# Summing two node tables on TensorE instead of VectorE in one stage of a graph network kernel

## What is computed

```
h = jnp.maximum(_layernorm(x, axis=-1), 0.0)
x = x + _L2_gnn_ref(h, edge_attr_32, edge_index, ...)

# in _L2_gnn_ref
proj_edge = (node_attr @ W_node)[edge_neigh]
m_node = segment_sum(proj_edge * (edge_attr @ W_edge), edge_center, num_segments=num_nodes)
cat = concatenate([node_attr @ W_center_node, m_node], axis=-1)
h_node = _layernorm(cat @ W_concat_node, ln_weight, ln_bias)
```

## Time and profile before

| what | value |
|---|---|
| median of three runs | 5954.6 us |
| the profiled execution | 5969.23 us, its span 5967.4 us |
| the stage's first and last sum on DVE | 4326.0 and 4697.8 us into the span |
| PE, DVE, ACT, POOL busy, of the whole span | 3748.6, 3959.9, 2012.0, 3039.3 us |

### The profile page before, as it was taken

One profiled execution on the slowest core, in us unless ns is written; L12 is line 12 of the kernel. 1 busy time (PEld: TensorE's weight loads), 2 busy tenths in 40 slices (PEclk: granted clock), 3 DMA queues, 4 the chain that ended last, 5 costly groups with the idle time before them and its releaser, 6 DMA issues. The chain is left out here.

```text
span 5967.4 us, 85405 instructions
## 1 busy us (share of the span) xinstructions
PE 3748.6 (63%) x16668; PEld 2531.9 (42%) x16668; DVE 3959.9 (66%) x12622; ACT 2012.0 (34%) x4449; POOL 3039.3 (51%) x2764
## 2 busy tenths in 40 slices
PE   0788883333599985579965566666400199889830
PEld 0566662332367764544455545555300044334310
DVE  8555556887388863654455555656488788888856
ACT  0555542333122221235565632222144333333310
POOL 0655534777676600000077767777700367777730
PEclk9888885555799998999967778888855599999975
DMA  6677766776455545877677767777588511111149
GB/s 228 151 174 173 172 159 192 219 217 176 125 132 144 142 161 170 276 246 229 219 243 231 227 170 130 131 130 128 88 280 271 156 31 39 43 46 47 49 162 375
DMA packets 986574, 996.40 MB, mean 167 GB/s; under 512 B 210641, under 2 KB 648417, under 8 KB 986163
## 3 DMA queue, kind: packets, MB, share of 16 engines
q1 hardware_dynamic: 676899, 628.12, 37.1%
q0 software_dynamic: 131904, 146.31, 12.6%
q10 hardware_dynamic: 177488, 218.95, 10.3%
HBM read 560.95 MB, written 466.16 MB: 172 GB/s over the span
## 5 line engine op out<-in xcount | busy, mean ns | idle before, releaser
L709 POOL DMA_INDIRECT at_first_table<-n_h,n_first_edge x784 | 811.5, 1035 | 1247.3 <-ACT n_h L277 901.1
L2495 PE MATMUL e_m<-e_by_rel,rel_w 128*128 128x512 f32 x1568 | 718.3, 613 | 0.0
L701 POOL DMA_INDIRECT e_xs<-x_table,e_idx x392 | 377.6, 963 | 516.0 <-POOLq L2385 396.8
L701 POOL DMA_INDIRECT e_x<-x,e_idx x392 | 408.2, 1041 | 371.8 <-DMA e_idx<-idx_table 261.3
L701 POOL DMA_INDIRECT e_hs<-h_table,e_idx x392 | 423.3, 1080 | 170.3 <-issue 110.9
L2409 DVE SCALAR_TENSOR_TENSOR e_by_rel<-e_y,e_part_t 128x512 f32<-128x512 f32 x784 | 476.0, 678 | 31.4 <-PE e_y L2510 24.0
L709 POOL DMA_INDIRECT rel_sum_table<-e_res,e_again x392 | 392.6, 1001 | 148.6 <-issue 125.2
L2495 PEld LDWEIGHTS e_m<-e_by_rel,rel_w 128*128 128x128 f32 x1568 | 302.6, 198 | 346.6 <-issue 346.6
L277 ACT ACTIVATE n_h<-n_x,n_norm_shift,n_norm_rstd 128x128 f32<-128x128 f32 x784 | 321.8, 482 | 327.1 <-issue 266.2
L1014 PE MATMUL n_m<-n_mean,n_pick 128*128 128x129 f32 x784 | 204.7, 442 | 356.2 <-DVE n_pick L1079 352.7
L2487 PE MATMUL e_t<-ident,e_part 128*128 128x128 f32 x392 | 70.1, 307 | 561.0 <-ACT e_part L277 442.6
(11 more groups left out here) (373 smaller groups left out, 10428.9 us busy)
## 6 DMA issues: line engine op xcount, KB each, us to landing
x_table<-n_x ACTq DMA_DIRECT2D x294, 256.0 KB
n_x<-x_table SPq DMA_DIRECT2D x294, 256.0 KB
e_hd<-at_first_table SPq DMA_DIRECT2D x196, 256.0 KB
mean_runs_table<-e_packed SPq DMA_DIRECT2D x196, 130.0 KB
n_mean<-mean_runs_table SPq DMA_DIRECT2D x392, 65.0 KB
at_first_table<-prep_zero ACTq DMA_DIRECT2D x1, 25088.0 KB
e_edge<-edge128T SPq DMA_DIRECT2D x98, 256.0 KB
e_keep<-col_tab_table SPq DMA_DIRECT2D x196, 128.0 KB
```

What stands on the lines that cost most here:

```text
L701: pool.indirect_dma_start(out=tile[:, t, :], out_offset=None, in_=table, in_offset=bass.IndirectOffsetOnAxis(ap=idx[:, col + t:col + t + 1 ...
L709: pool.indirect_dma_start(out=table, out_offset=bass.IndirectOffsetOnAxis(ap=idx[:, t:t + 1], axis=0), in_=tile[:, t, :], in_offset=None, ...
L2495: ins = pe.matmul(flat(at(ps_m, u - 6)), k.rel_w[:, r, :], at(by_rel, u - 6)[:, r, :], start=(r == 0), stop=(r == RELS - 1))
```

## The change

The sum moves from DVE to PE. For each step PE multiplies the identity with `low` and then with `high` and accumulates both products in one bank of PSUM (`ps_z`, four banks of 128 x 512 float32, one for each of four steps). DVE's statistics and ACT's scaled copies read that bank. `z` in SBUF is gone. The bank of step i-4 is free when ACT has made its `zn`; the `low` and `high` buffers are free when PE's second product is done (`z_done`). DVE's order is new: `zw`, then statistics and moments, then `x3`, then reciprocal and shift. `zn` has three buffers instead of two. All four engine programs use `each_step` instead of `run_steps`.

```
-        z, z_ready = ph.made("z", [P, TILES, D], 4)
-        zn, zn_ready = ph.made("zn", [P, TILES, D])
+        zn, zn_ready = ph.made("zn", [P, TILES, D], 3)
...
+        z_done = ph.sem("z_done")
+        ps_z = [ph.ps(f"z{u}") for u in range(SLOTS)]
@@ sync
-                        sp.wait_ge(z_ready, i - 3)
+                        sp.wait_ge(z_done, i - 3)
...
-            run_steps(sp, body, S, 3)
+            each_step(body, S, 3)
@@ tensor (new)
+                if live(i, S):
+                    pe.wait_ge(at(low_in, u), moved(i, u))
+                    if begun(i - 4):
+                        pe.wait_ge(zn_ready, i - 3)
+                    pe.matmul(flat(at(ps_z, u)), k.ident[:, :], flat(at(low, u)), start=True, stop=False)
+                    pe.wait_ge(at(high_in, u), moved(i, u))
+                    pe.matmul(flat(at(ps_z, u)), k.ident[:, :], flat(at(high, u)), start=False, stop=True
+                              ).then_inc(z_done, 1)
+            each_step(body, S, 0)
@@ vector
                     dve.wait_ge(zn_ready, j + 1)
+                    if begun(j - 2):
+                        dve.wait_ge(x3_ready, j - 1)
                     dve.tensor_tensor(zw <- zn * ln_w_rep).then_inc(zw_ready, 1)
+                if live(i, S):
+                    dve.wait_ge(z_done, i + 1)
+                    norm.moments_of(dve, at(ps_z, u), i, u)
+                if live(j, S):
                     wait x2_in, x3_out, zw_ready
                     dve.tensor_tensor(x3 <- zw + x2).then_inc(x3_ready, 1)
-                if live(i, S):
-                    dve.wait_ge(at(low_in, u), moved(i, u))
-                    dve.wait_ge(at(high_in, u), moved(i, u))
-                    if begun(i - 4):
-                        dve.wait_ge(zn_ready, i - 3)
-                    dve.tensor_tensor(z <- low + high).then_inc(z_ready, 1)
-                    dve.wait_ge(z_ready, i + 1)
-                    norm.moments_of(dve, at(z, u), i, u)
-            run_steps(dve, body, S, 3)
+            each_step(body, S, 3)
@@ scalar
-                    if begun(j - 2):
-                        act.wait_ge(zw_ready, j - 1)
-                    norm.apply(act, at(zn, u), at(z, u - 2), ACT.Identity, j, u - 2).then_inc(zn_ready, 1)
+                    if begun(j - 3):
+                        act.wait_ge(zw_ready, j - 2)
+                    norm.apply(act, at(zn, j), at(ps_z, u - 2), ACT.Identity, j, u - 2).then_inc(zn_ready, 1)
...
-            run_steps(act, body, S, 4)
+            each_step(body, S, 4)
```

More of the change, by code:

```diff
@@ L2271, in body, with _ @@
                     sp.dma_start(flat(at(x2, u - 3)), rows_of(scratch["x2"], j)).then_inc(at(x2_in, u - 3), 16)
-            run_steps(sp, body, S, 3)
+            each_step(body, S, 3)
+        @block.tensor
+        def _(pe):
+            def body(i, u):
+                if live(i, S):
[7 more added lines that the diff above has]
+            each_step(body, S, 0)
         @block.vector
@@ L2279, in body @@
                     dve.wait_ge(zn_ready, j + 1)
-                    dve.tensor_tensor(at(zw, u - 3)[:, :, :], at(zn, u - 3)[:, :, :], k.ln_w_rep[:, :, :], ALU.mult
+                    if begun(j - 2):
+                        dve.wait_ge(x3_ready, j - 1)
+                    dve.tensor_tensor(at(zw, j)[:, :, :], at(zn, j)[:, :, :], k.ln_w_rep[:, :, :], ALU.mult
                                       ).then_inc(zw_ready, 1)
-                    dve.wait_ge(at(x2_in, u - 3), moved(j, u - 3))
+                if live(i, S):
+                    dve.wait_ge(z_done, i + 1)
+                    norm.moments_of(dve, at(ps_z, u), i, u)
+                if live(j, S):
+                    dve.wait_ge(at(x2_in, j), moved(j, j))
                     if begun(j - 4):
-                        dve.wait_ge(at(x3_out, u - 3), moved(j - 4, u - 3))
+                        dve.wait_ge(at(x3_out, j), moved(j - 4, j))
                     dve.wait_ge(zw_ready, j + 1)
-                    dve.tensor_tensor(at(x3, u - 3)[:, :, :], at(zw, u - 3)[:, :, :], at(x2, u - 3)[:, :, :], ALU.add
+                    dve.tensor_tensor(at(x3, j)[:, :, :], at(zw, j)[:, :, :], at(x2, j)[:, :, :], ALU.add
                                       ).then_inc(x3_ready, 1)
-                if live(i, S):
-                    dve.wait_ge(at(low_in, u), moved(i, u))
-                    dve.wait_ge(at(high_in, u), moved(i, u))
-                    if begun(i - 4):
-                        dve.wait_ge(zn_ready, i - 3)
-                    dve.tensor_tensor(at(z, u)[:, :, :], at(low, u)[:, :, :], at(high, u)[:, :, :], ALU.add
-                                      ).then_inc(z_ready, 1)
-                    dve.wait_ge(z_ready, i + 1)
-                    norm.moments_of(dve, at(z, u), i, u)
                 j = i - 1
```

## The result

| | median | lowest to highest | runs |
|---|---|---|---|
| before | 5957.0 us | 5951.74 to 5968.38 | 6 |
| after | 5861.6 us | 5842.52 to 5873.99 | 6 |

The ratio is 0.9835, with an interval of 0.9815 to 0.9854: 95.4 us by the medians, where 88.6 was forecast and 5866 us as the time. The profiled execution of after took 5842.52 us, its span 5840.7.

A forecast was written before the change was run, and what follows sets the result against it. DVE's own instruction order was taken to bound the stage. (3.833 - 2.89) x 97 = 91.5 us, less 2.9 for the head, gives 88.6 us off the 5954.6 us median: 5866 us, range 5848 to 5877.

The forecast's parts named there:

- The bound: Gated node stage before the change: DVE sets the pace by its own instruction order, 3.833 us a step.
- my sign of being wrong: Outside the changed stage: if the other stages move, the prediction is wrong altogether; no size given.
- DVE's step: DVE in the changed stage: distances between starts sum to 2.79 us a step, from 3.833 before.
- Its three parts: DVE's 101 us over 97 steps: 14 from writing out, 17 from the new order, 70 from the sum.
- Statistics from PSUM: DVE's four statistics a step: reading PSUM instead of SBUF costs nothing, with 0.24 us a step as the other end.
- the rival: DVE's statistics: PSUM reads cost 0.24 us a step, 23 us over the stage, time 5889 us; chance 0.13.
- PE: PE's two products a step: 1.73 us at 2.4 GHz, hidden under DVE's 2.79; mean granted clock near 0.9.
- The slower-than-before rival: PE in the stage: low clock and exposed weight loads, 4.08 us a step, 27 us lost, 5982 us; chance 0.03.
- The queues: SP's load queue: loads have about three steps less 1 us, some 7 us, so waiting for PE costs nothing.
- The DMA engines: Transfers in the stage: next bound at 2.61 to 2.74 us a step, so 0.10 added, making the step 2.89.
- The rival's row: DMA share 0.95 at 305 GB/s, behind the case of DMA binding at 3.44 us a step, 5919 us; chance 0.10.
- Head and tail: Stage's ends: first statistics wait for four slow records, 2.9 us more; the tail keeps its form.

## Why the prediction was right, step by step

**The bound.** Right. Before and after, DVE's instructions follow each other with nothing between them, and three experiments (no weight product, three banks, four products) show at which point that ends. Other stages moving was my sign of being wrong. The profiled execution had this stage begin 31 us earlier, but the medians agree with the stage alone, and `relation_edges` takes 958.9 us for 957.9.

**DVE's step.** 2.79 forecast, 2.83 in mid-stage, 2.810 as the mean. The 0.04 came from taking the distances out of a step in the opening; the kernel before, written out, has 0.06 more in mid-stage. As the forecast took a mean over the whole stage for before and the opening's step for after, the error didn't cancel; that the mean lies 0.02 under mid-stage halved it, which is luck.

**Its three parts.** By the stage's length, in the order of the edits: writing out 8.9 us (forecast 14), order 19.4 (17), sum 67.0 (70). The sum of the three is 95.3; forecast were 101 less 9.7 for the DMA engines and 2.9 for the head. The writing out was the term mis-sized as a share of itself, by taking the difference between the whole stage and the opening's step as the loop's cost. Its size also isn't its own: from the changed kernel's side the loops cost 19.8 us and the old order 24.7. So "which part brings how much" has no single answer, and the forecast of the loop's share holds only for one order of the edits. The 24.7 contain the 4 us of long steps.

**Statistics from PSUM.** I took nothing, with 0.24 us a step as the other end. Statistics to moments is 1.07 us from PSUM and 1.05 to 1.06 from SBUF; the median record is 281 ns against 276. Over the stage that is 1 to 2 us, where the rival had 23. L2409's distances were the right row, and L1867's duration the wrong one: a duration contains what overlaps with the next instruction. The Trainium skill, "VectorE: DVE Perf Modes", section "The TRN2 errata", by which I had estimated 0.26 us a step, is not borne out here: the trace has 0.02. My reason for excluding a gain, the same element count, isn't a good one: ACT's copies, with the same count, became shorter from PSUM, 457 ns against 478.

**PE.** Two products take 4453.76 - 4451.81 = 1.95 us from first start to last end, hidden as forecast, and 4.44 us lie between the start of a bank's filling and its use, for which I had 4.5. The clock was better than my mean near 0.9: 1.00 in every stretch from the opening to PE's last product. It changes nothing in the sum. That it would rise and stay was a choice between rows of both kinds, not a derivation, and PE's busy share didn't decide: 28.08 of 38 us is 74% and 41.59 of 60 is 69% at 1.00 here, while 13.79 of 20, also 69%, had been at 0.50. The Trainium skill, "TensorE: Matmul & The Clock Gate", section "HAM oscillation", has waits between bursts bring the clock down, but its case has waits for transfers that are longer than the bursts between them. Pauses of 0.88 us in each step of 2.83 did not bring it down. I had read the section as a rule against any pause. PE's pauses in this stage are shorter than its bursts in every run, so the section's case is neither shown nor refuted. The slower-than-before rival needed weight loads that stand exposed at the lower clock; in the opening two records take 1.71 us (4299.43 - 4297.72, the second pair), 0.85 each, so nothing is exposed.

**The queues.** Right. No load was late; the queue's wait is now for `x3`.

**The DMA engines.** The step that failed in part: the allowance of 0.10 us a step for two limits so close, 9.7 us, wasn't needed, and no row had given it a size. The DMA engines' own step is 2.69 us by the kernel without the weight product, between my two numbers (2.61 and 2.74), and DVE's 2.83 isn't lengthened by anything: its distances are those of its own instructions. 0.14 us of room in 2.8 was enough. The rival's row, a share of 0.95 at 305 GB/s, I had put down to smaller transfers. That was wrong: the kernel with four products has 0.94 at 305 with the very transfers of this stage. The share doesn't grow with the traffic here. It is 0.86 at 272 GB/s, 0.94 at 305, 1.02 at 374 and 1.05 at 402, and only the last of these was a bound, so a share near 1 isn't one by itself.

**Head and tail.** 2.9 us forecast for the head, 3.6 measured to the first `zw`. The timeline of after (SP's first issue, PE's first start, DVE's first statistics):

```profile
4291.71 0.33 SPq L2264 DMA_DIRECT2D n_low<-sum_table  x1
...
4295.85 2.07 PE L2282 MATMUL n_z<-n_low,ident 128*128 128x512 f32 x2 [42.03 <-DMA n_low<-sum_table]
...
4297.72 1.92 PE L2284 MATMUL n_z<-n_high,ident 128*128 128x512 f32 x2
...
4299.67 0.89 DVE L238 BATCH_NORM_STATS2 n_norm_stats<-n_z 128x6 f32<-128x128 f32 x4 [43.45 <-PE n_z L2284]
```

From PE's start to the statistics it is 3.82 us, for 3.6 forecast, and PE's first start comes 0.7 later behind the first issue than DVE's first sum did before (4.1 and 3.4 us). The tail is 0.8 shorter.

**The sum.** Forecast were (3.833 - 2.89) x 97 = 91.5, less 2.9. Measured are (3.822 - 2.810) x 97 = 98.1, less 3.6 for the head and plus 0.8 from the tail: 95.3. The 6.7 us between are the allowance for DMA, 9.7 too much; against it stand the 0.02 by which the mean step is longer than 2.79 (1.9 us) and the 0.011 by which the old one is shorter than 3.833 (1.1 us).

## What to carry to other kernels

Where one engine runs without a wait, read its step as distances between starts in the middle of the stage, not in its opening. An edit is worth the distances that it takes out, until the next engine or the DMA engines need as much. How far away those limits are can be found with one kernel each: one that takes work off the bound, or adds it to the next engine. An `x3` that doesn't stand behind what it reads, 0.2 us a step, was as good as a fifth of the gain and needs no other engine. Don't carry "write it out" or "use the idle engine" over without a run: one cost 24 us in other stages, the other stretched a small instruction of the bound sixfold.

## What the runs showed of the hardware beyond this

- A loop cost more than its visible gap, and more in the kernel with the shorter steps: 0.094 us a step with steps of 3.7 us, 0.20 with steps of 2.8. The Trainium skill, "Runtime: NRT & Kernel Launch", section "Instruction fetch mechanics", has kernels prefer full unrolling because a taken branch whose target isn't among the pages already fetched stalls the engine. Whether that was so for these loops no run shows. In this stage written-out steps were indeed faster, by 9 and 20 us; in four other stages together they were not, 24 us lost.
- Written-out steps have a cost of their own: in two kernels one step in eight of this stage is 0.31 to 0.35 us longer, in after none is, with the same instructions.
- A 128x512 product on GpSimd takes 1.38 us beside DVE, and one of DVE's small instructions beside it goes from 0.16 to 1.02 us and ends with it, while the reciprocal beside it keeps its 0.17.
- The same kernel before took 5954.2 us on the first chip, 6497.2 on the second and 5940.3 on the third. In the profiles of the second, `relation_edges` takes some 1215 us by its `e_xb` sums where it takes 959 on the first, while the stage of this document shows no such difference. A comparison is only good on one chip.
